# A convolution's zeroing, round change and skip rebuilt, and a first projection started ahead of its rates

## The chip, the core and the metric

One core of a Trainium2 chip runs the whole program. Its engines are TensorE (PE, with its weight loads shown as PEld), VectorE (DVE), ScalarE (ACT), GpSimd (POOL) and SyncE (SP), which issues all DMAs here. The metric is the device time of one execution in microseconds, the median of the runs. PE's granted clock is shown as a share of 2.4 GHz.

## What is computed

Cut to what matters here: 16 images of 64 channels and 32 x 32 pixels go through a two-sided recurrent convolution of 32 steps, then through a state-space scan, then through a mixture of experts.

```python
# convolution: 32 steps for a left and a right side, f = 32 features
pre = sigmoid(s2s(h, w, b, shift) + x @ w_i2s)   # o, fg, ig, g = split(pre, 4)
c = fg * c + ig * g
h = o * tanh(c)
...
x1 = x + (lh + shift_down(rh)) @ w_skip + b_skip
# scan: layernorm of x1, projections xs, z, delta, Bv, Cv
state = exp(delta * A) * state + delta * Bv * xs
y = (state @ C) * silu(z) @ W_out
```

## The kernel before

**The convolution** (`conv_phase`) keeps four streams s: two sides times two halves of the batch group, four images (GROUP) in each. `rows[s]` holds 64 channels of state (rows 0 to 63, the previous features twice, shifted) above 64 channels of x. There are two rounds, each of 8 images, 32 steps and four streams per step. For each stream PE computes the four gates of two chunks (512 pixels) with 16 matmuls a chunk in quarters of its columns (L165), ACT applies the sigmoid (L207) and tanh (L214), POOL and DVE update the cell (L247, L270, L277), DVE writes the features (L285) and SP copies them into `rows` (L136). After 32 steps the skip runs: for each of 8 images and 2 chunks PE multiplies both sides' features with `skip_w` (L180, L182) into rows 64 to 127 of one PSUM bank, DVE adds bias and x (L307), SP stores (L143).

Before the first round POOL and DVE zero all of `rows` and `feat` (L228, L229, L253, L254); at the start of each round, the first one too, SP loads x (L129) in the order 0, 2, 1, 3, POOL zeroes the state rows of streams 0, 2 and 1 (L237, L240), DVE the cells and stream 3 (L263, L264), and PE waits for all of it once (L151). The loops over rounds are loops of the machine (Fori) on every engine.

**The scan phase** (`build_scan`) starts when all engines have left the convolution. The projection of one batch is a list of 16 stages (STAGES, L505): MEAN, VARIANCE, two OWN, two RATES, two READOUT, STEPS_OF, OWN_TOKENS and ENTERS twice, two Z. In each, PE fills one PSUM bank `work_ps` (`fill`), ACT drains it (`drain`), and where the value is split into bf16 parts, ACT takes the first and second part and POOL the remainders (L1111, L1115); SP stores the parts (`store_stage`). The two buffers `parts` are used by turns: ACT's first part of a stage waits (`parts_out`) until the stores of the last stage but one of that kind have landed. Batch 0 is projected ahead of everything; the later ones run inside the scan of the batch before. Ahead of batch 0's projection the rates A are turned (L728), split into three bf16 parts by ACT and DVE (L919 to L923, L1211, L1214), stored and loaded back (L611, L620). POOL and DVE zero the scan's tiles (L1070 to L1074, L1206 to L1209). When the last stage's parts are stored, SP loads the first span (`load`, L622), and the scan begins (DVE L1231).

All order between engines comes from semaphores written out by hand; each engine's own order is the program's.

## Time and profile before

| what | us |
|---|---|
| median of 3 runs | 6596.51 (6596.5 to 6597.06) |
| the profiled execution | 6594.51 |
| its span, first to last instruction | 6592.7 |
| PE busy | 6199.5 (94%) |
| DVE busy | 6099.6 (93%) |
| ACT busy | 4496.3 (68%) |
| POOL busy | 2566.4 (39%) |

The busy shares are means over phases with different limits, so they are read phase by phase. The convolution ends at about 1886 us, the scan phase at about 6504 us; the experts take the rest. A busy PE counts matmuls that overlap.

### The profile page before, as it was taken

How to read it: one execution, taken by the hardware profiler on the slowest of the kernel's cores; microseconds unless marked ns; L12 is line 12 of the kernel's file. 1: busy time of each engine (PE TensorE's matmuls, PEld its weight loads, DVE VectorE, ACT ScalarE, POOL GpSimd, SP SyncE). 2: the span in 40 equal slices, each digit the busy share in tenths (PEclk: the TensorE clock that was granted, in tenths of full speed). 3: DMA queues.
4: the chain of work that ended last, by engine and by line, in shares of the span. 5: the costliest groups of instructions: out<-in, count | busy, mean ns of one | idle time of the engine just before them, and what ended most of it. 6: DMA issues, size and time to landing. Idle time of an engine off the chain costs nothing. (4 is left out here: it accounts for less than half of the span.)

```text
span 6592.7 us, 155525 instructions
## 1 busy us (share of the span) xinstructions
PE 6199.5 (94%) x52289; PEld 4017.0 (61%) x52289; DVE 6099.6 (93%) x3714; ACT 4496.3 (68%) x9595; POOL 2566.4 (39%) x7016
## 2 busy tenths in 40 slices
PE   8999989999959999999999999999999999999996
PEld 3666634567726666666666666666666666666654
DVE  7888878888839999999999999999999999999995
ACT  7888858888836666666666666666666666666662
POOL 5555545555532333333333333333333333333321
PEclk9999999999979999999999999999999999999997
DMA  6666666666641221212212122221212212222114
GB/s 144 154 154 154 154 145 154 154 154 154 155 105 44 49 56 40 65 47 52 55 41 63 42 59 49 47 58 38 68 46 51 55 41 64 48 53 50 45 32 127
DMA packets 904175, 538.20 MB, mean 82 GB/s; under 512 B 695565, under 2 KB 813997, under 8 KB 903597
## 3 DMA queue, kind: packets, MB, share of 16 engines
q1 hardware_dynamic: 903597, 531.10, 34.5%
q8 instruction: 289, 4.73, 0.3%
q14 instruction: 289, 2.37, 0.1%
HBM read 142.32 MB, written 107.35 MB: 38 GB/s over the span
## 5 line engine op out<-in xcount | busy, mean ns | idle before, releaser
L1231 DVE TENSOR_TENSOR_SCAN states<-decay,enter_ps 128x1024 f32<-128x1024 f32 x2048 | 4471.9, 2262 | 86.3 <-PE enter_ps L801 73.6
L987 ACT ACTIVATE decay<-rate_ps 128x512 f32<-128x512 f32 (+1 forms) x4096 | 2221.7, 594 | 344.0 <-PE rate_ps L787 149.0
L801 PEld LDWEIGHTS enter_ps<-s_steps,s_tokens 128*128 128x128 bf16 x16384 | 1602.8, 129 | 1358.6 <-DVE states L1231 1063.0
L801 PE MATMUL enter_ps<-s_steps,s_tokens 128*128 128x128 bf16 x16384 | 2142.1, 310 | 238.1 <-DVE states L1231 228.3
L787 PE MATMUL rate_ps<-s_wide,s_decays 128*128 128x256 bf16 x8192 | 1318.5, 283 | 4.8 <-DMA s_wide<-rates_dram 4.5
L247 POOL TENSOR_TENSOR entered<-gates 128x512 f32<-128x512 f32 x512 | 901.1, 1760 | 887.5 <-ACT gates L207 887.5
L1167 POOL TENSOR_TENSOR product<-decay,states 128x16 f32<-128x16 f32 x1920 | 465.8, 243 | 1788.0 <-ACT decay L987 1784.4
L994 ACT COPY enter_ps<-at_first 128x16 f32<-128x16 f32 x1920 | 337.5, 176 | 1188.0 <-PE enter_ps L801 1134.2
L831 PE MATMUL y_ps<-states,spread 128*32 128x512 f32 x8192 | 1090.3, 604 | 2.4 <-issue 2.4
L165 PE MATMUL pre<-rows,weights_left 128*32 128x512 f32 x8192 | 909.1, 595 | 36.0 <-POOL rows L240 23.8
L787 PEld LDWEIGHTS rate_ps<-s_wide,s_decays 128*128 128x128 bf16 x8192 | 903.5, 118 | 63.4 <-issue 6.1
L285 DVE TENSOR_TENSOR feat<-gates,squashed 128x512 f32<-128x512 f32 x512 | 904.0, 1766 | 1.4 <-ACT squashed L214 1.4
L165 PE MATMUL pre<-rows,weights_right 128*32 128x512 f32 x8192 | 904.9, 593 | 0.0
L165 PEld LDWEIGHTS pre<-rows,weights_left 128*32 128x32 f32 x8192 | 541.6, 109 | 381.6 <-issue 217.8
L165 PEld LDWEIGHTS pre<-rows,weights_right 128*32 128x32 f32 x8192 | 549.0, 109 | 334.5 <-issue 175.6
L207 ACT ACTIVATE gates<-pre,biases_left 128x512 f32<-128x512 f32 x1024 | 620.4, 689 | 133.9 <-PE pre L165 133.9
L207 ACT ACTIVATE gates<-pre,biases_right 128x512 f32<-128x512 f32 x1024 | 620.7, 689 | 125.0 <-PE pre L165 125.0
L270 DVE TENSOR_TENSOR forgot<-gates,cell 128x512 f32<-128x512 f32 x512 | 356.7, 697 | 260.1 <-ACT gates L207 259.9
L1172 POOL TENSOR_TENSOR at_first<-at_first,product 128x16 f32<-128x16 f32 x1920 | 426.5, 222 | 309.9 <-ACT at_first L1002 309.9
L277 DVE TENSOR_TENSOR cell<-forgot,entered 128x512 f32<-128x512 f32 x512 | 347.4, 678 | 2.3 <-POOL entered L247 2.3
L214 ACT ACTIVATE squashed<-cell 128x512 f32<-128x512 f32 x512 | 330.8, 646 | 5.6 <-DVE cell L277 5.6
L831 PEld LDWEIGHTS y_ps<-states,spread 128*32 128x32 f32 x8192 | 161.6, 107 | 219.6 <-issue 219.6
(136 smaller groups left out, 2487.9 us busy)
## 6 DMA issues: line engine op xcount, KB each, us to landing
rows<-feat SPq DMA_DIRECT2D x1024, 132.0 KB, 2.4
rows<-feat SPq DMA_DIRECT2D x512, 128.0 KB, 2.4
s_steps<-steps_dram SPq DMA_DIRECT2D x4096, 8.0 KB
rows<-feat SPq DMA_DIRECT2D x512, 127.8 KB, 2.4
s_wide<-rates_dram SPq DMA_DIRECT2D x1024, 32.0 KB, 1.9
s_tokens<-tokens_dram SPq DMA_DIRECT2D x2048, 16.0 KB, 2.1
rates_dram<-parts SPq DMA_DIRECT2D x64, 384.0 KB, 3.3
steps_dram<-parts SPq DMA_DIRECT2D x64, 384.0 KB, 3.5
```

Source lines behind the costliest of these rows:

```text
L165: mm = pe.matmul(pre[c][32 * q:32 * q + 32, g, :], weights[side(s)][:, 32 * g:32 * g + 32], image(rows[s][:, q, :], MARGIN + CIMG * c), st ...
L207: a = act.activation(gates[k % GATE_RING][:, g, :], pre[k % CHUNKS][:, g, :], ACT.Sigmoid, bias=biases[side(k // CHUNKS)][:, g:g + 1])
L247: pool.tensor_tensor(entered[c][:, :], gates[k % GATE_RING][:, 2, :], gates[k % GATE_RING][:, 3, :], ALU.mult).then_inc(entered_ready, 1)
L270: dve.tensor_tensor(forgot[c][:, :], gates[k % GATE_RING][:, 1, :], cell[s][:, BANK * c:BANK * c + BANK], ALU.mult).then_inc(forgot_ready, 1)
L285: dve.tensor_tensor(image(feat[s][:, :], CIMG * c), gates[k % GATE_RING][:, 0, :].rearrange("p (h w) -> p h w", w=SIDE), squashed[c][:, :] ...
L787: mm = pe.matmul(rate_ps[h][:, QUAD * q:QUAD * q + QUAD, :], decays[:, g, 2 * h + q, :], wide[s][:, g, :, :], start=True, stop=True)
L801: mm = pe.matmul(out.rearrange("p h l -> p l h"), tokens[s][:, k, :], steps[s][:, k, :, d:d + half], start=True, stop=True)
L831: mm = pe.matmul(y_ps[32 * j:32 * j + REACH, :].rearrange("p (r d) -> p d r", r=QUAD), spread[s][:, at:at + REACH], steps_of.rearrange("p ...
L987: act.activation(decay[i][:, half, at:], rate_ps[h][:, :, at:], ACT.Exp).then_inc(decay_ready, 1)
L1167: pool.tensor_tensor(product[i][:, :], decay[g % RING][:, :, 0], states[set_of(c - 1)][:, mine, SPAN - 1], ALU.mult).then_inc(product_read ...
L1172: pool.tensor_tensor(at_first[set_of(c)][:, mine], at_first[set_of(c)][:, mine], product[i][:, :], ALU.add).then_inc(added, 1)
L1231: dve.tensor_tensor_scan(out, factor, term, 0.0, ALU.mult, ALU.add).then_inc(scanned, 1)
```

## The change

In the convolution: SP loads stream 0's x first, then the weights, then the other x, without waiting for any zeroing; the round loop on SP is written out. Before the first round only the margins of the x rows and the state rows are zeroed, and the round's zeroing stands at the end of the round instead of its start: the cells before the skip's evacuations, state rows of streams 0 and 2 after half of them, of 1 and 3 after all. PE waits for each stream's zeroing with a semaphore of its own, in the step loop. The skip takes an image's two chunks into the two column halves (rows 64 to 127 and 0 to 63) of two banks, with the matmuls of the two interleaved. ACT does one small sigmoid at the start of each round.

In the scan phase: mean_w and batch 0's x are loaded first; PE fills MEAN before it turns the rates and before it waits for the other weights; ACT splits the rates after the first drain; all the scan's zeroing goes to DVE, behind the rates, and is waited for where the scan begins; batch 0's stages use `work_ps` and `rate_ps[0]` by turns, so that a fill waits for the drain of the last stage but one (RATES and VARIANCE for all drains).

```diff
@@ -81,7 +81,11 @@
...
-        weights_in, zeroed, state_zeroed = sem("weights_in"), sem("zeroed"), sem("state_zeroed")
+        warm = sb("warm", [128, 1])
+        weights_in, zeroed, cells_zeroed, margins_zeroed = (
+            sem("weights_in"), sem("zeroed"), sem("cells_zeroed"), sem("margins_zeroed"))
+        state_zeroed = [sem(f"state_zeroed{s}") for s in range(STREAMS)]
...
+        def skip_ps(k, c):
+            at = CH * (1 - c)
+            return pre[k % 2][at:at + CH, c, :]
...
+            def load_x(r, s):
+                if r:
                     sp.wait_ge(x1_ready, START + r * SKIPS - (1 - half(s)) * SKIPS // 2)
-                    src = x_pad[bass.ds((r * 2 + half(s)) * GROUP, GROUP), :, :].rearrange("q c p -> c q p")
...
+                first = (r * 2 + half(s)) * GROUP
+                sp.dma_start(rows[s][CH:128, :, MARGIN:MARGIN + IMG], x_pad[first:first + GROUP, :, :].rearrange(
+                    "q c p -> c q p")).then_inc(x_in[s], DMA)
+            def load_weights():
+                for d, s in ((weights[0], w_left), (weights[1], w_right), (biases[0], bias_left),
+                             (biases[1], bias_right), (skip_w[0], w_skip_left), (skip_w[1], w_skip_right)):
+                    sp.dma_start(d[:, :], s).then_inc(weights_in, DMA)
+                sp.dma_start(skip_b[CH:128, :], b_skip).then_inc(weights_in, DMA)
+            for r in range(ROUNDS):
+                if r == 0:
+                    load_x(r, 0)
+                    load_weights()
+                    for s in (1, 2, 3):
+                        load_x(r, s)
+                else:
+                    for s in (0, 2, 1, 3):
+                        load_x(r, s)
...
+            pe.wait_ge(margins_zeroed, START + 1)
             with pe.Fori(0, ROUNDS) as r:
-                pe.wait_ge(state_zeroed, START + (r + 1) * 2)
-                pe.sem_inc(passed, 1)
...
+                        pe.wait_ge(state_zeroed[s], START + r + 1)
...
-                for k in range(SKIPS):
-                    h, q, c = k // (GROUP * CHUNKS), k // CHUNKS % GROUP, k % CHUNKS
-                    if q == 0 and c == 0:
+                for k in range(SKIPS // CHUNKS):
+                    h, q = k // GROUP, k % GROUP
+                    if q == 0:
                         for s in (h, 2 + h):
                             pe.wait_ge(rows_in[s], START + (r + 1) * STEPS * MOVES * DMA)
-                    if k >= 4:
-                        pe.wait_ge(x1_ready, START + r * SKIPS + k - 3)
-                    out = pre[k // 2 % 2][CH:128, k % 2, :]
-                    pe.matmul(out, skip_w[0][:, :], image(rows[h][:, q, :], MARGIN + 1 + CIMG * c),
-                              start=True, stop=False)
-                    pe.matmul(out, skip_w[1][:, :], image(rows[2 + h][:, q, :], MARGIN - 1 + CIMG * c),
-                              start=False, stop=True).then_inc(skip_ready, 1)
+                    if k >= 2:
+                        pe.wait_ge(x1_ready, START + r * SKIPS + (k - 1) * CHUNKS)
+                    for c in range(CHUNKS):
+                        pe.matmul(skip_ps(k, c), skip_w[0][:, :], image(rows[h][:, q, :], MARGIN + 1 + CIMG * c),
+                                  start=True, stop=False)
+                    for c in range(CHUNKS):
+                        pe.matmul(skip_ps(k, c), skip_w[1][:, :], image(rows[2 + h][:, q, :], MARGIN - 1 + CIMG * c),
+                                  start=False, stop=True).then_inc(skip_ready, 1)
...
+                act.activation(warm[:, :], biases[0][:, 0:1], ACT.Sigmoid)
...
+            pool.memset(rows[0][0:CH, :, :], 0.0).then_inc(state_zeroed[0], 1)
+            pool.memset(rows[1][0:CH, :, :], 0.0).then_inc(state_zeroed[1], 1)
+            pool.wait_ge(state_zeroed[1], START + 1)
             for s in range(2):
-                pool.memset(rows[s][:, :, :], 0.0)
...
-                pool.wait_ge(x1_ready, START + r * SKIPS - SKIPS // 2)
-                pool.sem_inc(passed, 1)
-                for s in (0, 2):
-                    pool.memset(rows[s][0:CH, :, :], 0.0)
-                pool.wait_ge(x1_ready, START + r * SKIPS)
-                pool.sem_inc(passed, 1)
-                pool.memset(rows[1][0:CH, :, :], 0.0).then_inc(state_zeroed, 1)
...
+                pool.wait_ge(x1_ready, START + (r + 1) * SKIPS - SKIPS // 2)
+                pool.sem_inc(passed, 1)
+                for s in (0, 2):
+                    pool.memset(rows[s][0:CH, :, :], 0.0).then_inc(state_zeroed[s], 1)
+                pool.wait_ge(x1_ready, START + (r + 1) * SKIPS)
+                pool.sem_inc(passed, 1)
+                pool.memset(rows[1][0:CH, :, :], 0.0).then_inc(state_zeroed[1], 1)
...
+            for s in range(STREAMS):
+                dve.memset(rows[s][CH:128, :, 0:MARGIN], 0.0)
+                z = dve.memset(rows[s][CH:128, :, MARGIN + IMG:], 0.0)
+            z.then_inc(margins_zeroed, 1)
+            dve.memset(rows[2][0:CH, :, :], 0.0).then_inc(state_zeroed[2], 1)
+            dve.memset(rows[3][0:CH, :, :], 0.0).then_inc(state_zeroed[3], 1)
...
                 z = dve.memset(feat[s][:, :], 0.0)
             z.then_inc(zeroed, 1)
+            def zero_cells():
+                for s in range(STREAMS):
+                    z = dve.memset(cell[s][:, :], 0.0)
+                z.then_inc(cells_zeroed, 1)
+            zero_cells()
...
-                for s in range(STREAMS):
-                    dve.memset(cell[s][:, :], 0.0)
-                dve.memset(rows[3][0:CH, :, :], 0.0).then_inc(state_zeroed, 1)
-                dve.wait_ge(state_zeroed, START + (r + 1) * 2)
-                dve.sem_inc(passed, 1)
...
+                zero_cells()
...
-                        in0=pre[k // 2 % 2][CH:128, k % 2, :].rearrange("p (h w) -> p h w", w=SIDE),
+                        in0=skip_ps(k // CHUNKS, c).rearrange("p (h w) -> p h w", w=SIDE),
...
+                dve.wait_ge(x1_ready, START + (r + 1) * SKIPS)
+                dve.sem_inc(passed, 1)
+                dve.memset(rows[3][0:CH, :, :], 0.0).then_inc(state_zeroed[3], 1)
...
+        def bench(b, n):
+            return work_ps if b or n % 2 == 0 else rate_ps[0][:, :, :].rearrange("p h l -> p (h l)")
...
+            def load_x(b):
+                sp.wait_ge(centred_ready, SCAN0 + b)
+                sp.sem_inc(passed, 1)
+                sp.dma_start(px[:, :], by_half(x1_dram)[b, :, :, :].rearrange("k c l -> (k c) l")).then_inc(x_in, DMA)
+            sp.dma_start(wmean[:, :], mean_w).then_inc(mean_in, DMA)
+            load_x(0)
+            sp.dma_start(rate_t[:, :], a_t).then_inc(consts_in, DMA)
+            sp.dma_start(ident[:, :], identity).then_inc(consts_in, DMA)
+            for d, s in ((wdelta, w_delta), (wc, w_c)):
...
-            load_x(0)
-            sp.dma_start(rate_t[:, :], a_t).then_inc(consts_in, DMA)
-            sp.dma_start(ident[:, :], identity).then_inc(consts_in, DMA)
...
-            sp.wait_ge(pool_zeroed, SCAN0 + 1)
-            sp.wait_ge(vector_zeroed, SCAN0 + 1)
+            sp.wait_ge(decays_zeroed, SCAN0 + 1)
...
+            sp.wait_ge(vector_zeroed, SCAN0 + 1)
...
-            pe.wait_ge(consts_in, SCAN0 + 2 * DMA)
-            pe.wait_ge(y_zeroed, SCAN0 + 1)
-            pe.transpose(y_ps[:, 0:128], rate_t[:, :], ident[:, :]).then_inc(turned, 1)
-            pe.wait_ge(weights_in, SCAN0 + WEIGHTS * DMA)
-            pe.wait_ge(by_place_set, SCAN0 + 1)
...
+                work_ps = bench(b, n)
+                pe.wait_ge(drained, stages_to(b, n) if b or kind in (RATES, VARIANCE) else stages_to(b, max(n - 1, 0)))
...
+            pe.wait_ge(mean_in, SCAN0 + DMA)
             for n in range(len(STAGES)):
                 fill(0, n)
+                if n == 0:
+                    pe.wait_ge(consts_in, SCAN0 + 2 * DMA)
+                    pe.wait_ge(y_zeroed, SCAN0 + 1)
+                    pe.transpose(y_ps[:, 0:128], rate_t[:, :], ident[:, :]).then_inc(turned, 1)
+                    pe.wait_ge(weights_in, SCAN0 + WEIGHTS * DMA)
+                    pe.wait_ge(by_place_set, SCAN0 + 1)
                 fill_inverse(0, n)
+            pe.wait_ge(drained, stages_to(1, 0))
...
-            pe.wait_ge(pool_zeroed, SCAN0 + 1)
...
-            act.wait_ge(turned, SCAN0 + 1)
-            act.copy(rate[:, :], y_ps[:, 0:128]).then_inc(rate_moved, 1)
-            act.wait_ge(rate_moved, SCAN0 + 1)
-            act.copy(rate_parts[:, 0, :], rate[:, :]).then_inc(rate1, 1)
-            act.wait_ge(left1, SCAN0 + 1)
-            act.copy(rate_parts[:, 1, :], rate_left[:, :]).then_inc(rate2, 1)
-            act.wait_ge(vector_zeroed, SCAN0 + 1)
...
+            def split_rates():
+                act.wait_ge(turned, SCAN0 + 1)
+                act.copy(rate[:, :], y_ps[:, 0:128]).then_inc(rate_moved, 1)
+                act.wait_ge(rate_moved, SCAN0 + 1)
+                act.copy(rate_parts[:, 0, :], rate[:, :]).then_inc(rate1, 1)
+                act.wait_ge(left1, SCAN0 + 1)
+                act.copy(rate_parts[:, 1, :], rate_left[:, :]).then_inc(rate2, 1)
...
+                if n == 0:
+                    split_rates()
+            act.wait_ge(vector_zeroed, SCAN0 + 1)
...
-            pool.memset(steps[0][:, :, :, :], 0.0)
-            pool.memset(decays[:, :, :, :], 0.0)
-            for s in range(SETS):
-                pool.memset(room[s][:, INNER * SPAN:], 0.0)
-                z = pool.memset(spread[s][:, :], 0.0)
-            z.then_inc(pool_zeroed, 1)
-            pool.wait_ge(pool_zeroed, SCAN0 + 1)
...
+            pool.wait_ge(vector_zeroed, SCAN0 + 1)
...
+            dve.memset(decays[:, :, :, :], 0.0).then_inc(decays_zeroed, 1)
...
-            for i in range(RING):
-                dve.memset(decay[i][:, :, :], 0.0)
-            for s in range(SETS):
-                dve.memset(wide[s][:, :, :, :], 0.0)
-            dve.memset(steps[1][:, :, :, :], 0.0).then_inc(vector_zeroed, 1)
...
+            for i in range(RING):
+                dve.memset(decay[i][:, :, :], 0.0)
+            for s in range(SETS):
+                dve.memset(wide[s][:, :, :, :], 0.0)
+                dve.memset(steps[s][:, :, :, :], 0.0)
+                dve.memset(room[s][:, INNER * SPAN:], 0.0)
+                z = dve.memset(spread[s][:, :], 0.0)
+            z.then_inc(vector_zeroed, 1)
+            dve.wait_ge(consts_in, SCAN0 + 2 * DMA)
+            rows = ident[:, :].rearrange("p (j a e) -> p j a e", j=4, a=2)
+            for a in range(2):
+                p = dve.tensor_scalar(place[:, SPAN * a:SPAN * a + SPAN].rearrange("p (j e) -> p j e", e=16), rows[:, :, a, :],
+                                      0.5, None, ALU.mult)
+            p.then_inc(placed, 1)
...
```

## Rows read from the trace of the kernel before

**Rows 1.** Busy time of each engine (instructions) in three stretches, granted clock, DMA share, GB/s.
```profile
1000.00:1800.00 800.00, 800.00 (x7424) 509.25 (x7416) 692.07 (x696) 682.40 (x1160) 408.16 (x233) 1.00 0.68 154
1921.10:1965.50 44.40, 28.65 (x64) 14.67 (x64) 0.00 (x0) 14.83 (x27) 18.29 (x16) 0.50 0.38 123
2000.00:6500.00 4500.00, 4256.55 (x35050) 2830.82 (x35047) 4456.01 (x2041) 2933.83 (x6939) 1592.38 (x6453) 1.00 0.21 50
```

**Rows 2.** Timeline of the start: start us, us, engine, line, operation, idle before.
```profile
2.23 0.39 SPq L121 DMA_DIRECT2D weights_left<-w_left  x1
...
19.40 3.62 POOL L240 MEMSET rows<- 64x4240 f32 x1
...
23.76 8.76 PE L165 MATMUL pre<-rows,weights_left 128*32 128x512 f32 x64 [23.76 <-POOL rows L240]
...
29.20 1.28 ACT L207 ACT_TABLE_LOAD   x1 [29.20 <-PE pre L165]
...
30.50 4.74 ACT L207 ACTIVATE gates<-pre,biases_left 128x512 f32<-128x512 f32 x8
...
32.97 7.10 PE L165 MATMUL pre<-rows,weights_left 128*32 128x512 f32 x64 [0.46 <-ACT gates L207]
```

**Rows 3.** x's loads in the first 45 us; DMA traffic of 20 to 34.
```profile
DMA to landing us min/median/max: 8.1/14.9/21.5
...
DMA packets 702, 2.83 MB, mean 202 GB/s; under 512 B 32, under 2 KB 32, under 8 KB 702
```

**Rows 4.** Timelines by engine of the first skip and the round change.
```profile
918.03 1.94 PE L180 MATMUL pre<-rows,skip_w_left 128*64 128x512 f32 x2 [8.39 <-DMA rows<-feat]
...
957.80 9.35 PE L165 MATMUL pre<-rows,weights_left 128*32 128x512 f32 x64 [10.41 <-DMA rows<-x_pad]
968.48 7.08 PE L165 MATMUL pre<-rows,weights_left 128*32 128x512 f32 x64 [1.33 <-DMA rows<-x_pad]
...
921.79 0.76 DVE L307 SCALAR_TENSOR_TENSOR x<-pre,skip_b,rows 64x512 f32<-64x512 f32 x1 [5.28 <-PE pre L182]
...
947.43 0.76 DVE L307 SCALAR_TENSOR_TENSOR x<-pre,skip_b,rows 64x512 f32<-64x512 f32 x1 [0.96 <-PE pre L182]
...
953.53 3.59 DVE L264 MEMSET rows<- 64x4240 f32 x1 [0.82 <-issue]
...
949.46 3.07 SPq L129 DMA_DIRECT2D rows<-x_pad  x4
```

**Rows 5.** Timelines: the second skip's end, the scan phase's first, an output product.
```profile
1882.89 0.76 DVE L307 SCALAR_TENSOR_TENSOR x<-pre,skip_b,rows 64x512 f32<-64x512 f32 x1 [0.96 <-PE pre L182]
...
1886.56 0.11 POOL L1067 MEMSET power<- 128x8 f32 x1 [36.87 <-POOLq L65]
...
2342.56 1.08 PE L851 MATMUL stage_ps<-gated,wout 128*64 128x512 f32 x4
```

**Rows 6.** Timelines by engine of the scan phase's front.
```profile
1913.07 1.84 PE L745 MATMUL stage_ps<-wmean,square 128*128 128x2 f32 x8 [10.68 <-POOL square L1089]
...
1921.08 2.07 PE L752 MATMUL stage_ps<-normed,win 128*128 128x512 f32 x2 [2.02 <-POOL normed L1103]
...
1909.36 0.23 DVE L1211 TENSOR_TENSOR rate_left<-rate,rate_parts 128x128 f32<-128x128 f32 x1
...
1982.42 2.29 DVE L1231 TENSOR_TENSOR_SCAN states<-decay,enter_ps 128x1024 f32<-128x1024 f32 x1 [71.91 <-PE enter_ps L801]
...
1963.60 0.36 SPq L577 DMA_DIRECT2D tokens_dram<-parts  x1
```

**Rows 7.** Groups by line in 1921:1966; DMA issues in 1890:1985, median us to landing.
```profile
L1115 POOL TENSOR_TENSOR parts<-rest,parts 128x512 bf16<-128x512 f32 x6 | 6.9, 1154 | 4.4 <-ACT parts L973 4.4
...
L961 ACT COPY moved<-stage_ps 128x512 f32<-128x512 f32 x7 | 4.1, 588 | 4.5 <-PE stage_ps L757 4.5
...
px<-x_dram SPq DMA_DIRECT2D x2, 256.0 KB, 2.7
...
steps_dram<-parts SPq DMA_DIRECT2D x2, 256.0 KB, 3.8
```

30 lines of the change are left out of this document (10 added, 20 removed).

## The prediction, made before the changed kernel ran

> **What bounds the kernel now.** I read the busy shares by stretch first [rows 1]. In the convolution's steady part PE is busy 800.00 of 800 us at a granted clock of 1.00 (2.4 GHz): PE sets the pace. In the scan DVE is busy 4456 of 4500 us. Between these lies the first batch's projection, 44.4 us in which no engine is busy two thirds of the time and the granted clock is 0.50 (1.2 GHz). So the two long stretches can't be shortened by this change, which leaves their instructions alone but for one wait; what it can move are the serial pieces between them. The timelines of those give four: the start [rows 2, 3], the round change with its skip [rows 4], the same skip again before the scan [rows 5], and the scan's front [rows 6, 7]. All four are serial, so what one loses or gains shifts everything behind it.
>
> **1. The start.** PE's first matmul is at 23.76, released by POOL's last zeroing (19.40 + 3.62) [rows 2]. That chain goes: both engines zero whole rows, SP waits for them, x is loaded, and only the round's own zeroing, repeated over the same rows, lets PE go. After the change, SP loads x for stream 0 first. Its present first issue is at 2.23 [rows 2]; five more semaphores are set up in front of it, each below 0.1 us, so 2.5. The earliest x load of the four took 8.1 us from issue to landing and the last 21.5 [rows 3], so the four share the queues one behind the other, about 5.3 us each at the 202 GB/s shown. Stream 0 lands at 10.6. The seven weight loads are queued behind it: 0.2 MB at the same rate, about 1 us, ending at 11.6 to 12.5. The zeroing in front of PE is now one half-height memset on POOL (3.62, over by 4.4) and the margins on DVE: PE starts at about **11.8**, on weights instead of on POOL. Streams 1, 2, 3 land at about 17, 22, 28; PE wants them at 20.4, 27, 34 (its first pieces are 8.6 and then 6.9 us long [rows 2]). DVE's zeroing (14,700 elements a partition at 3.59 per 4240 [rows 4], 12.4 us, and gaps between eight memsets) ends near 18, before the first gates at 11.8 + 5.4 + 2.4 = 19.6. The table load of 1.28 us [rows 2] moves ahead of PE's first result; now PE's second stream starts 9.21 us after the first because it waits for ACT; without the load it would be bound by its own 8.6, so 0.6 comes back and not 1.28. Gain 12.0 + 0.5 = **12.5**, ends 10.5 and 13.5.
>
> **2. The first skip.** It runs from 918.03; its first evacuation is at 921.79 and its 16th ends at 948.19, one each 1.71 us, each waiting for PE [rows 4]. PE computes the two halves of an image in turn, in 64 of its columns. The change puts them on different column halves and interleaves them. The nearest row is the scan's output product, which writes both column halves too: four matmul instructions of this size in 1.08 us [rows 5], where the skip needs 1.71 for four. So two halves should cost PE 1.71 instead of 3.42. The other engine becomes nearly as tight: a group's two evacuations need 2 x 0.76, and group k waits for those of group k-2. That cycle is 1.93 (8 instructions) + 1.52 + 0.14 (a wait on another engine) + whatever gap lies between two evacuations, for two groups: 1.8 each without a gap; with the largest gap DVE shows with nothing to wait for, 0.82 [rows 4], 2.2. I take 1.8, as the gap is shown before a memset of another shape. The x1 stores have a ring of four, land 2.3 us after issue and need a pace of 1.7 per group or slower: they just fit. The first group stays at the low clock (3.43 for what then takes 1.71). So group 7 starts at 918.0 + 3.4 + 6 x 1.8 = 932.3 and the last evacuation ends at 935.8: gain **12.3** (9.5 to 13).
>
> A rule of the Trainium skill speaks of the evacuations: by "VectorE: DVE Perf Modes", section "Two Vector instructions with no wait between them", an instruction whose PSUM input starts in another quadrant than the last one's is held until all earlier ones have ended. The new evacuations alternate between partitions 64 and 0, so all would be held. No row shows it; it would only fill the gap that the range above already contains.
>
> **3. The round change.** Now: last evacuation 948.19, x loads issued at 949.46, PE at 957.80 released by the landing, second stream at 968.48 released by the third landing [rows 4]. The change takes the zeroing out of the way (cells in the 5 us in which DVE waits for the skip's first product, streams 0 and 2 during the skip's second half, streams 1 and 3 afterwards, 3.6 to 4.7 us against 9.6 until x lands), but PE waits for the load and not for it. So nothing of the zeroing is gained here, and the table load is not gained either: PE's second stream waits for a landing 10.68 us after the first, whatever ACT does. All is shifted by the skip's 12.3, **0** beside it (-0.5 to +1.5).
>
> **4. The second skip and the end of the phase.** The same 12.3. But the moved zeroing is now at the end of every round, also of the last. Now the phase ends with the last store's landing: evacuation over at 1883.65, scan phase at 1886.56, 2.9 us [rows 5]. After: DVE's stream 3 memset comes behind the last evacuation, 0.4 for the wait, up to 0.82 of idle and 3.59 [rows 4], so 4.7, and about 0.5 for the barrier: 5.1. Cost 2.2 (1 to 3). Net **10.1**.
>
> **5. The scan's front to the second stage.** Now all weights, then x, then the rates' constants are loaded; PE turns the rates first, and ACT can drain the first mean only after DVE's zeroing (rate_left at 1909.36), so PE's variance matmul comes at 1913.07, 26.5 us into the phase [rows 6]. After: mean_w and x are loaded first, and PE's mean starts about 8 us in (x issued at 5.3, landing 2.7 later [rows 7]). Drain, centring and squaring end at 13.2. In PE's order the wait for the remaining weights now stands between mean and variance. The last of 14 loads is issued at 11.2, lands 2.2 later, the by_place copy takes 0.3: variance at **13.9**. Gain 12.6. Behind that wait nothing else is queued but the transpose's successors; ACT's second rate copy waits for DVE, over by 14.4, before the variance is there at 15.7. SP's 19 decay loads are finished 24 us in, the first parts store is due at 33. From variance to the first OWN product the chain is unchanged, 8.0 us [rows 6]. DVE's zeroing, 15,600 elements a partition, 13.2 us at the same rate and 17 with gaps, now runs 15 to 32 us in; it is wanted at 60. Its cost is nil unless it slows POOL beside it; no row has a POOL operation beside a DVE memset, the nearest is POOL's memset of [rows 2], at 3.62 no slower than without company: 0, at worst 2.
>
> **6. Two banks.** OWN at zero, the last third part (what SP stores and the loads wait for) ends now 42.4 after it (OWN at 1921.08, store of the last part at 1963.60) [rows 6]. With two banks PE fills the next stage while ACT drains. I laid the stages out from [rows 7]: PE 2.05 per stage at the low clock, 1.71 back to back; ACT 0.59 a copy; POOL 1.15 each. OWN1 starts at 1.7 and ends its drain at 4.4; the rates stages still wait for all drains, 4.55 and 7.85; the readouts are drained at 13.4 and 13.9; STEPS_OF 0 is cast at 15.6 and its third part is ready at 19.9; ENTERS 0 is stored at 25.0. Then a new wait: STEPS_OF 1 takes the parts buffer whose three stores were issued from 20.0 on, the last landing 3.8 after its issue [rows 7], at 24.7, where ACT would be free at 23.8. Its chain goes on through 27.0 (rest), 28.1 (ENTERS 1 drained), plus the 5.8 that its six operations on ACT and POOL, 0.6 to 1.3 each with the hand-overs, take now: 33.9. Gain **8.6**; 6 if POOL is slowed, 9.5 if the stores land sooner. PE is by then busy nearly without gaps, and a rise of the clock would give under 1 us, since ACT, POOL and the stores hold the chain. From the store to the first scan nothing changes (1963.60 to 1982.42, 18.8 us of store, landing and SP's issues).
>
> **7. The added wait in the step loop.** PE waits once more for each stream, 256 times, and DVE once per round. Behind it on PE is the stream's first matmul, behind that ACT, POOL and DVE. Today two or three waits stand at the same place and PE has no idle time there [rows 1], so I take 0. If nothing hid it, it would be some 0.1 us, 26 in all.
>
> **Sum.** 12.5 + 12.3 + 0 + 10.1 + 12.6 + 8.6 = 56.1 us. The profiled execution took 6594.51 (span 6592.7 and 1.8 around it): 6538.4. The median of the runs, 6596.51, lies 2.0 higher, so I forecast **6540.5**.
>
> **Rivals.** (a) The column halves don't overlap. Then both skips keep 1.71 per half and 24.6 is lost: 6565. For it: the weights change with each matmul; against it the 1.08 us of [rows 5]. The Trainium skill would have it so: "TensorE: Matmul & The Clock Gate", section "Part 3: Packing small matmuls — row/col tiling", says that a weight load overlaps running matmuls only when its row group differs, and here all use the full rows. The trace disagrees: in the four-column-group matmuls of the step loop PE is busy without idle time although each has its weight load [rows 1]. Chance 0.03. (b) The projection gains less (POOL slowed by DVE's memsets, or stores that hold both parts buffers): 12 instead of 21, 6550. Chance 0.1. (c) It ends slower: the added wait empties PE's queue, so that each stream's first matmul starts only when the last one has ended. That costs one matmul's time less its pitch, 0.6 - 0.1 = 0.5 us, 256 times: 128 us, 6668. It decides from 0.27 us per wait on. Against it: the waits there already don't do so. Chance 0.02. (d) The same wait is hidden in part, 5 to 25 us: 6546 to 6566, 0.04. (e) The convolution's part does not do what it says, because the weights land late behind x or the phase's end costs more: 6545, within my range, 0.06.
>
> **Chances and range.** The forecast, 6533 to 6549, has 0.75. Adding up the ends of the terms, with (b) and part of (d), gives **6530 to 6558** for 8 in 10. A measurement of this kernel can tell 0.2% (13 us) from no change; all cases but (c) and the worst of others are beyond it: faster 0.96, same 0.02, slower 0.02.
>
> **What would show it.** PE's first matmul near 11.8, released by a weights DMA. In each skip, pairs of evacuations 0.8 apart, every 1.8 us, and 18 us from first skip matmul to last evacuation. x landings 8 us after the stores as now. The phase's end 5 us after the last evacuation, with a DVE memset in it. Variance 14 us and OWN 22 us into the scan phase, the last parts store at 56, the first scan at 75. PE without idle time in the step loop. It would be wrong if PE idled at stream changes, if evacuations stayed 1.7 us apart, or if the gain in the projection were taken by waits for parts stores.

## The result and the profile after

The changed kernel takes 6540.72 us (median of 4 runs, 6538.69 to 6541.35) against 6596.78 us for the kernel before on the same chip (4 runs, 6596.5 to 6597.44): a ratio of 0.9916, 95% interval 0.9904 to 0.9928, so 56.1 us less. The profiled execution took 6541.35 us, with a span of 6539.6. The profiled span before was 6592.7, so the two traces differ by 53.1 us and not by 56.1: the one of before lay 2.3 us under its median, the one of after 0.6 above. Everything below that is read from traces adds up to 53, not 56.

The table follows the difference through the program. A mark is a moment in both traces, in us from the span's start. The last column is what the stretch ending at the mark gave. Each column is one trace: how far such marks scatter is told at the head of the experiments, and a difference below about 1 us in a stretch is not a finding.

| mark | before | after | ahead by | this stretch |
|---|---|---|---|---|
| PE's first matmul | 23.76 | 13.66 | 10.10 | 10.10 |
| first skip, first matmul | 918.03 | 907.18 | 10.85 | 0.75 |
| first skip, last evacuation over | 948.19 | 925.51 | 22.68 | 11.83 |
| second skip, first matmul | 1853.71 | 1831.46 | 22.25 | -0.43 |
| second skip, last evacuation over | 1883.65 | 1850.15 | 33.50 | 11.25 |
| first work of the scan phase | 1886.56 | 1855.09 | 31.47 | -2.03 |
| variance matmul | 1913.07 | 1868.88 | 44.19 | 12.72 |
| last parts store | 1963.60 | 1910.30 | 53.30 | 9.11 |
| first scan | 1982.42 | 1929.06 | 53.36 | 0.06 |

**The start**, against [rows 2, 3]. The first four lines are from the timeline, the next two from the DMA issues of the first 16 us (size, and median time from issue to landing), the last the one x load issued in the window 2.4 to 3.2:

```profile
2.50 0.76 SPq L133 DMA_DIRECT2D rows<-x_pad  x1
...
6.34 0.51 SPq L140 DMA_DIRECT2D skip_b<-b_skip  x1
...
12.96 1.28 ACT L240 ACT_TABLE_LOAD   x1 [12.96 <-DMA skip_b<-b_skip]
...
13.66 2.79 PE L186 MATMUL pre<-rows,weights_left 128*32 128x512 f32 x12 [13.66 <-DMA skip_b<-b_skip]
...
weights_left<-w_left SPq DMA_DIRECT2D x1, 64.0 KB, 7.3
...
skip_b<-b_skip SPq DMA_DIRECT2D x1, 0.2 KB, 6.5
...
rows<-x_pad SPq DMA_DIRECT2D x1, 1056.0 KB, 8.0
```

PE is now released by a weights DMA and not by POOL. Stream 0's x is issued at 2.50 and takes 8.0, so it lands at 10.5; the last weight is issued at 6.34 and takes 6.5, for 0.2 KB. It lands at 12.8, and PE's first matmul follows 0.85 later. PE then runs 128 matmuls in a row, where it stood idle for 0.46 us before its second stream [rows 2].

**The first skip and the round change**, against [rows 4]. First the busy times by engine in three windows (columns as in [rows 1]), then lines of the timeline by engine:

```profile
905.00:912.00 7.00, 4.82 (x12) 1.66 (x14) 5.29 (x7) 1.44 (x2) 0.00 (x0) 0.51 0.84 193
912.00:926.00 14.00, 11.94 (x54) 3.26 (x50) 11.06 (x15) 0.00 (x0) 7.53 (x3) 1.00 0.62 133
926.00:935.00 9.00, 0.00 (x0) 0.00 (x0) 3.59 (x1) 0.00 (x0) 3.29 (x1) 0.67 0.94 192
...
907.18 1.98 PE L201 MATMUL pre<-rows,skip_w_left 128*64 128x512 f32 x4 [8.39 <-DMA rows<-feat]
...
914.78 1.08 PE L201 MATMUL pre<-rows,skip_w_left 128*64 128x512 f32 x4
915.70 1.03 PE L204 MATMUL pre<-rows,skip_w_right 128*64 128x512 f32 x4
...
915.02 1.54 DVE L342 SCALAR_TENSOR_TENSOR x<-pre,skip_b,rows 64x512 f32<-64x512 f32 x2 [0.29 <-PE pre L204]
916.75 1.54 DVE L342 SCALAR_TENSOR_TENSOR x<-pre,skip_b,rows 64x512 f32<-64x512 f32 x2 [0.20 <-PE pre L204]
...
935.33 9.01 PE L186 MATMUL pre<-rows,weights_left 128*32 128x512 f32 x64 [11.39 <-DMA rows<-x_pad]
946.02 7.08 PE L186 MATMUL pre<-rows,weights_left 128*32 128x512 f32 x64 [1.68 <-issue]
```

A group of four matmuls now takes 1.08 us as in the output product of [rows 5], and the evacuations come in pairs (1.54 for two). From the third pair (915.02) to the eighth (923.97) they are 1.6 to 2.0 us apart, 1.79 in the mean. Until 912 the granted clock is 0.51. PE's next start still waits for x, and its second stream comes 10.69 us after the first (10.68 before).

**The end of the convolution and the front of the scan phase**, against [rows 5, 6]: lines of the timeline, then two windows.

```profile
1847.00 3.15 DVE L342 SCALAR_TENSOR_TENSOR x<-pre,skip_b,rows 64x512 f32<-64x512 f32 x4 [0.51 <-PE pre L204]
...
1851.21 3.59 DVE L350 MEMSET rows<- 64x4240 f32 x1 [1.06 <-issue]
1855.09 0.11 POOL L1119 MEMSET power<- 128x8 f32 x1 [1.16 <-POOLq L65]
...
1868.88 1.84 PE L784 MATMUL rate_ps<-wmean,square 128*128 128x2 f32 x8 [3.37 <-DVE by_place L1249]
...
1891.81 0.59 ACT L991 CAST parts<-stage_ps 128x512 bf16<-128x512 f32 x1 [2.14 <-DMA rates_dram<-parts]
1900.94 0.59 ACT L991 CAST parts<-rate_ps 128x512 bf16<-128x512 f32 x1 [1.08 <-DMA steps_dram<-parts]
...
1910.30 0.36 SPq L623 DMA_DIRECT2D tokens_dram<-parts  x1
...
1000.00:1780.00 780.00, 780.00 (x7236) 467.78 (x7231) 674.70 (x679) 664.90 (x1130) 398.11 (x226) 1.00 0.68 154
1868.00:1911.00 43.00, 24.13 (x88) 14.89 (x88) 16.61 (x19) 15.86 (x30) 20.50 (x18) 0.73 0.44 138
```

A DVE memset now stands between the last evacuation and the scan phase. Variance is released by `by_place`, the last consumer of the weight loads. In the projection ACT waits twice for a store of parts that it wants to overwrite. The granted clock is 0.73 there; it was 0.50 [rows 1].

### The profile page after: what moved, and what is told of

Read it like the earlier page. It is cut to its first block and busy times, and to the rows that moved or that the text cites. A ratio compares the mean times of both kernels' runs of the same rounds, so it can differ in the third digit from the quotient of the medians.

```text
span 6539.6 us, 155482 instructions
## 1 busy us (share of the span) xinstructions
PE 6169.2 (94%) x52289; PEld 3694.8 (56%) x52289; DVE 6112.0 (93%) x3734; ACT 4495.5 (69%) x9597; POOL 2554.8 (39%) x7010
## 3 DMA queue, kind: packets, MB, share of 16 engines
q14 instruction: 289, 2.37, 0.1%
## 5 line engine op out<-in xcount | busy, mean ns | idle before, releaser
L186 PEld LDWEIGHTS pre<-rows,weights_left 128*32 128x32 f32 x8192 | 389.4, 109 | 524.2 <-issue 439.4
L186 PEld LDWEIGHTS pre<-rows,weights_right 128*32 128x32 f32 x8192 | 389.4, 109 | 494.0 <-issue 401.4
L1214 POOL MEMSET decay<- 128x16 f32 x1920 | 242.3, 126 | 113.5
```

Of the source, the lines that this page charges most:

```text
L186: mm = pe.matmul(pre[c][32 * q:32 * q + 32, g, :], weights[side(s)][:, 32 * g:32 * g + 32], image(rows[s][:, q, :], MARGIN + CIMG * c), st ...
```

## The experiments

All medians are of timed runs of a kernel beside the kernel before on the same chip (whose medians were 6594.4 to 6596.8 in the five groups of runs). Where only 1 to 3 us are at stake I judge by marks in the trace. The reason is in the runs themselves: the stretch from the first scan to the end, which no experiment touches, took between 4607.9 and 4614.7 us in the fourteen traces.

Marks scatter too, by less. In the ten traces whose start is the changed kernel's, PE's first matmul comes at 13.66 to 14.54 us; the changed kernel's own trace has the earliest. From there to the first skip the thirteen traces of changed kernels take 893.5 to 895.3 us (before: 894.3), a skip that no experiment touched 17.3 to 18.9, and the eight with SP's loads of x and the skip as changed take 922.9 to 924.6 from the first skip's first matmul to the second's. So I count a stretch between two marks, and not a mark from the span's start, and call less than about 1 us scatter unless it comes back in several traces.

**E1: both chunks of an image in one column half.** The changed kernel with the skip's outputs in partitions 64 to 127 of both banks.

```diff
-            at = CH * (1 - c)
-            return pre[k % 2][at:at + CH, c, :]
+            return pre[k % 2][CH:128, c, :]
```

> The changed kernel, but both halves of an image are written to partitions 64 to 127 (two banks, matmuls still interleaved, evacuations still wait by groups). Theory: the skips' gain is the overlap of the two column halves on PE. Then a group costs PE 3.4 us again, each skip takes about 30 us from first matmul to last evacuation (18.3 and 18.7 in the changed kernel), and the time is 23 us above the changed kernel, about 6564. Rival: the gain came from the interleaving and the two buffers, not from the columns; then each skip stays below 22 us and the time rises by less than 8 us.

Measured: 6566.87 us (6564.46 to 6568.88), ratio 0.9957 (0.9943 to 0.9971). The timeline of its first skip, PE then DVE:

```profile
914.11 1.89 PE L200 MATMUL pre<-rows,skip_w_left 128*64 128x512 f32 x4
915.83 1.88 PE L203 MATMUL pre<-rows,skip_w_right 128*64 128x512 f32 x4
...
916.89 1.61 DVE L341 SCALAR_TENSOR_TENSOR x<-pre,skip_b,rows 64x512 f32<-64x512 f32 x2 [1.82 <-PE pre L203]
920.44 1.50 DVE L341 SCALAR_TENSOR_TENSOR x<-pre,skip_b,rows 64x512 f32<-64x512 f32 x2 [1.94 <-PE pre L203]
```

Four matmuls now start 1.72 apart from the next four, where the changed kernel has 0.86 to 0.92, and each pair of evacuations waits 1.8 to 1.9 us for PE. The skip, from first matmul to last evacuation, takes 31.1 us (908.03 to 939.13) in place of 18.3. The column halves are the whole of the skip's gain: by the marks 24.5 us for both rounds (31.1 and 30.4 us against 18.3 and 18.7); the medians differ by 26. The order of the matmuls is that of the changed kernel, and the skip of before took 30.2 us, so interleaving alone brought nothing. Whether the column halves would do it without interleaving was not run.

**E2: one bank for the stages.** All of batch 0's stages in `work_ps`, each fill behind the last drain.

```diff
-            return work_ps if b or n % 2 == 0 else rate_ps[0][:, :, :].rearrange("p h l -> p (h l)")
+            return work_ps
...
-                pe.wait_ge(drained, stages_to(b, n) if b or kind in (RATES, VARIANCE) else stages_to(b, max(n - 1, 0)))
+                pe.wait_ge(drained, stages_to(b, n))
```

> The changed kernel with batch 0's stages in one bank again, each fill waiting for all drains. Theory: two banks are worth what the trace shows between the first OWN product and the last parts store (42.5 us before, 33.4 after): the stretch is 42.5 again, the time 9 us above the changed kernel, about 6550. Rival: the stretch got shorter because PE's clock rose in it; then it is the clock and not the bank that matters, and the stretch stays below 38 us with the time less than 5 us up.

Measured: 6550.03 us (6549.16 to 6553.39), ratio 0.9935 (0.9918 to 0.9951). The window of its projection, and its last store:

```profile
1868.00:1920.00 52.00, 30.97 (x87) 18.08 (x88) 15.78 (x19) 15.93 (x29) 20.31 (x18) 0.50 0.37 115
...
1919.68 0.36 SPq L623 DMA_DIRECT2D tokens_dram<-parts  x1
```

From OWN (1877.16) to the last store are 42.5 us; before it was 42.5 too, after 33.4. So the two banks give 9.1 us, and the rest of the front nothing of it. The clock stays at 0.50, so the rise to 0.73 came with the two banks, and the 9.1 us hold what the clock gave: E2 takes both away together.

**E3: the small weights ahead of x in the scan phase's front.**

```diff
-            load_x(0)
-            sp.dma_start(rate_t[:, :], a_t).then_inc(consts_in, DMA)
-            sp.dma_start(ident[:, :], identity).then_inc(consts_in, DMA)
...
+            load_x(0)
+            sp.dma_start(rate_t[:, :], a_t).then_inc(consts_in, DMA)
+            sp.dma_start(ident[:, :], identity).then_inc(consts_in, DMA)
```

> The changed kernel with the scan phase's x and the rates' constants loaded behind all weights, as before the change; only mean_w stays in front. Theory: of the 12.7 us that the variance matmul comes earlier, the load order is worth the smaller part: x is issued 10.4 us in, lands at 13.1, and mean, drain, centring and squaring (5.2 us) end at 18.5 against 13.8 now, so plus 4.7 us, about 6545; the other 8 us come from ACT no longer waiting for DVE's zeroing. Rival: the load order is the whole gain, plus 12 us, about 6553.

Measured: 6545.06 us (6544.17 to 6546.05), ratio 0.9926 (0.9909 to 0.9943). In its timeline:

```profile
1868.53 2.07 PE L779 MATMUL stage_ps<-px,wmean 128*128 128x512 f32 x2 [19.59 <-DMA px<-x_dram]
...
1873.94 1.83 PE L784 MATMUL rate_ps<-wmean,square 128*128 128x2 f32 x8 [3.12 <-POOL square L1133]
```

Variance comes 23.4 us after the last evacuation (1850.52), against 18.7 in the changed kernel: 4.7 later, and it is now released by POOL's square instead of by `by_place`. So of the front's 12.7 us, 4.7 come from the order of the loads; the other 8.0 are left to what E3 keeps, the mean ahead of the rates and DVE's zeroing out of the way. I didn't separate those two.

**E4 and E4b: the added wait.** E4 has the wait for `state_zeroed` three times in the step loop. E4b takes it out of the loop and puts four waits ahead of the round.

```diff
                         pe.wait_ge(state_zeroed[s], START + r + 1)
+                        pe.wait_ge(state_zeroed[s], START + r + 1)
+                        pe.wait_ge(state_zeroed[s], START + r + 1)
```

> The changed kernel with the new wait in PE's step loop issued three times in a row, 512 more waits. Theory: PE's sequencer runs ahead of the matmuls, so the wait is free: same time within 1.5 us, about 6541, and no idle time of PE in the step loop. Rival: the wait costs what its issue takes, about 0.1 us each: plus 50 us, and then the change itself pays 25 us for it. Second rival: it empties the queue: plus 250 us.

> The changed kernel with TensorE's added wait taken out of the step loop and put once ahead of the round. Theory: the wait in the loop costs nothing, since three of it cost nothing: 6540 to 6541.5, TensorE busy 780.00 of 780 us between 1000 and 1780. Rival: one wait in the loop already costs what three do not add to, and without it the time falls below 6538.

Measured: E4 6540.07 us (6539.53 to 6546.17), E4b 6541.29 us (6538.19 to 6542.18), the changed kernel 6540.72. The same window of E4, then of E4b:

```profile
1000.00:1780.00 780.00, 780.00 (x7238) 482.57 (x7234) 674.89 (x679) 664.23 (x1131) 397.77 (x226) 1.00 0.68 154
```

```profile
1000.00:1780.00 780.00, 780.00 (x7236) 454.33 (x7232) 674.87 (x679) 664.96 (x1131) 397.67 (x226) 1.00 0.68 154
```

No wait in the loop, one or three: PE is busy throughout and does the same number of matmuls, to within 2 of 7236. The wait is free. Neither rival has anything left.

**E5: no zeroing after the last round.** The round loops of POOL and DVE written out, and left before the zeroing when no round follows.

```diff
-                zero_cells()
+                if r + 1 < ROUNDS:
+                    zero_cells()
...
+                if r + 1 == ROUNDS:
+                    break
```

> The changed kernel, with the zeroing of features and cells left out behind the last round (nothing reads them there). Theory: the zeroing at the phase end, 3.6 us on VectorE and GpSimd side by side behind the last evacuation (1850.15 to 1855.09 in the changed kernel's trace), is what the second skip gives back, so without it the scan phase starts 2 to 4.5 us earlier and the time is 2 to 4.5 us under the changed kernel's 6540.7: 6536 to 6539, and the stretch from the last evacuation to the first work of the scan phase falls from 4.9 to about 1.0 to 2.5 us. Rival: the phase end is bounded by SyncE's drain or the barrier and not by the zeroing; then the time stays within 1 us of 6540.7.

Measured: 6536.49 us (6530.19 to 6538.25), ratio 0.9908 (0.9891 to 0.9925). Its timeline at the end of the convolution:

```profile
1847.29 1.54 DVE L345 SCALAR_TENSOR_TENSOR x<-pre,skip_b,rows 64x512 f32<-64x512 f32 x2 [0.18 <-PE pre L204]
1851.55 0.11 POOL L1124 MEMSET power<- 128x8 f32 x1 [24.11 <-POOLq L65]
```

From the last evacuation's end (1848.83) to the scan phase's first work are 2.7 us, 4.9 in the changed kernel and 2.9 before. So the zeroing is what the second skip gives back, 2.2 us. The stretch didn't fall to 1.0 to 2.5 as I expected: it is what it was before, and what I read there as the last store's landing. The median is 4.2 lower, of which the trace explains half.

**E6: three buffers for parts.**

```diff
-        parts = [sb(f"parts{i}", [128, SPLITS, BANK], BF16) for i in range(2)]
+        parts = [sb(f"parts{i}", [128, SPLITS, BANK], BF16) for i in range(3)]
```

> The changed kernel with three buffers for the projection's parts in place of two. Theory: ScalarE's two waits for a part's store (2.14 us at 1891.81 and 1.08 us at 1900.94 in the changed kernel's trace) stand on the path from the last part to the first scan; with a third buffer they go, and the last tokens' store and the first scan come 2 to 3 us earlier: 6537.5 to 6539. Rival: the loads and matmuls behind it are next in line (a load of rates or steps, or TensorE at its low clock), and the time is 6540 to 6541, the waits having moved to another releaser.

Measured: 6539.04 us (6538.0 to 6541.41), ratio 0.9914 (0.9898 to 0.9931). In its trace:

```profile
1868.00:1911.00 43.00, 25.76 (x88) 14.49 (x88) 14.79 (x19) 15.85 (x30) 21.29 (x18) 0.66 0.47 146
...
1891.34 0.59 ACT L991 CAST parts<-stage_ps 128x512 bf16<-128x512 f32 x1 [0.82 <-PE stage_ps L796]
...
1908.97 0.36 SPq L623 DMA_DIRECT2D tokens_dram<-parts  x1
```

Both waits for stores are gone, 3.2 us of them, but from OWN (1876.66) to the last store are 32.3 us against 33.4: 1.1 came through. It is not scatter: the three traces with three buffers (E6, E9, E10) take 32.26 to 32.31, the nine with two buffers and two banks 33.0 to 34.5. In the place of the first wait stands one of 0.82 us for PE. Another 1.1 us were lost ahead of it: ACT drains the first readout 12.8 us after OWN and not 11.7, with the granted clock at 0.50 over the first 12 us behind OWN, where it is above 0.8 in the changed kernel. So the theory is right about the place and too high in size; most of the rest of the 3.2 us went to PE, as the rival has it.

**E7 and E8: the two loads that the new kernel waits for.** E8 issues the seven small weights from ACT and x from SP.

```diff
+            for d, s in ((weights[0], w_left), (weights[1], w_right), (biases[0], bias_left),
+                         (biases[1], bias_right), (skip_w[0], w_skip_left), (skip_w[1], w_skip_right)):
+                act.dma_start(d[:, :], s).then_inc(weights_in, DMA)
+            act.dma_start(skip_b[CH:128, :], b_skip).then_inc(weights_in, DMA)
```

> The changed kernel, with the seven small weight loads issued by ScalarE's queue at the start and the four of x by SyncE's. Theory: the first matmul (13.66 us) waits for the last weight, which lands 2.3 us after x because it stands behind it in one issuing queue; with two issuers the weights land with x or before it and the first matmul comes 1 to 1.5 us earlier: 6539 to 6540. Rival: the seven loads share the 16 DMA engines with x either way and x itself lands later by as much; the first matmul is at 13 to 14.5 us and the time at 6540.5 to 6542.

Measured: 6537.55 us (6536.85 to 6538.71), ratio 0.9912 (0.9896 to 0.9929). In its trace, issues first:

```profile
3.58 0.55 ACTq L217 DMA_DIRECT2D skip_b<-b_skip  x1
...
13.65 2.79 PE L178 MATMUL pre<-rows,weights_left 128*32 128x512 f32 x12 [13.65 <-DMA skip_b<-b_skip]
...
weights_left<-w_left ACTq DMA_DIRECT2D x1, 64.0 KB, 1.9
...
skip_w_right<-w_skip_right ACTq DMA_DIRECT2D x1, 32.0 KB, 7.0
...
skip_b<-b_skip ACTq DMA_DIRECT2D x1, 0.2 KB, 9.2
```

The median would have passed for my theory; the trace refutes it. The first five weights land in about 2 us. The last two, issued at 3.10 and 3.58, behind x's 2.51 but in another engine's queue, take 7.0 and 9.2 (a second load of x is issued at 3.32, between the two), and skip_b lands at 12.8 just as in the changed kernel. PE starts at 13.65 instead of 13.66. That is not quite nothing, since the changed kernel's 13.66 is the earliest of ten traces (the middle is 14.2) and E9 and E10, with the same edit, have 13.78 and 13.81: perhaps 0.4 us, not the 1 to 1.5 of the theory. The 3 us of the median are mostly the long part behind, 4607.85 us here, the shortest of the fourteen. So a small load behind a 1 MB load waits for most of it, whoever issues it. The Trainium skill says so in "DMA: Bandwidth & Descriptors", section "Issuing engines are not separate DMA queues": loads of different engines run on the same 16 DMA engines and interleave. This trace agrees that the issuer does not matter; of interleaving the last two loads saw little (skip_w_right lands at 10.1, x at 10.7). I had cost that queue by bytes alone.

E7 has the second round's x issued by ACT during the skip instead of by SP behind the skip's stores; for that PE waits for the last evacuation before it begins the round. The two kernels differ in the order of the four streams only, 0, 1, 2, 3 and 0, 2, 1, 3.

```diff
+                if r + 1 < ROUNDS:
+                    for s in (0, 1, 2, 3):
+                        act.wait_ge(x1_ready, START + (r + 1) * SKIPS - (1 - half(s)) * SKIPS // 2)
+                        first = ((r + 1) * 2 + half(s)) * GROUP
+                        act.dma_start(rows[s][CH:128, :, MARGIN:MARGIN + IMG], x_pad[first:first + GROUP, :, :].rearrange(
+                            "q c p -> c q p")).then_inc(x_in[s], DMA)
```

> The changed kernel, with the second round's x loaded from ScalarE's queue while the skip runs (streams in the order 0, 1, 2, 3), in place of SyncE's loads behind the round's end. Theory: TensorE's start of round 2 waits for x (first matmul at 935.33, 9.3 us after x is asked for at 926.02), and its second stream waits for its own x until 946.02. With the loads issued during the skip, the second stream's x is there about 10 us earlier, so round 2 gains 8.5 to 11 us: 6530 to 6532. Rival 1: the round's start is bounded by the zeroing and the barrier just as closely, and only 0 to 3 us are gained (6538 to 6541). Rival 2: x's 1 MB loads beside the skip slow the skip's own operands or evacuations, and half of the gain is given back (6535 to 6537).

> As the kernel with x loaded during the skip in the order 0, 1, 2, 3 (6534.75 us), but in the order 0, 2, 1, 3. Theory: in the new round the streams run in the order 0, 1, 2, 3, so with stream 1's x third in the queue its first step is held until the third landing, some 2.5 to 3 us later per load in the queue: 6536 to 6538. Rival: all loads land before they are needed, and the order makes no difference: 6534 to 6535.5.

Measured: with 0, 1, 2, 3 6534.75 us (6533.15 to 6537.14), ratio 0.9908 (0.9892 to 0.9925); with 0, 2, 1, 3 6537.08 us (6534.45 to 6543.26), ratio 0.991 (0.9894 to 0.9927). First lines of the former, then of the latter:

```profile
928.17 3.10 DVE L347 SCALAR_TENSOR_TENSOR x<-pre,skip_b,rows 64x512 f32<-64x512 f32 x4 [4.66 <-DMA x_dram<-x]
...
932.52 16.31 PE L183 MATMUL pre<-rows,weights_left 128*32 128x512 f32 x128 [6.92 <-issue]
```

```profile
929.27 0.76 DVE L347 SCALAR_TENSOR_TENSOR x<-pre,skip_b,rows 64x512 f32<-64x512 f32 x1 [6.75 <-DMA x_dram<-x]
...
935.17 15.95 PE L183 MATMUL pre<-rows,weights_left 128*32 128x512 f32 x128 [10.55 <-issue]
```

The second stream's wait is gone in both (128 matmuls in a row). But the skip itself is longer: its last four evacuations wait for the buffers that hold x on its way out, because these stores now move beside a 1 MB load. With one load beside them the wait is 4.66 us and the skip ends at 931.27; with two (streams 0 and 2 before the last stores) it is 6.75 and 1.6 more, and the skip ends at 933.92, against 925.51. From the first skip's first matmul to the second's the two take 917.2 and 921.5 us, against 922.9 to 924.6 in the eight traces with SP's loads: about 6 and 2 us less. So my second rival was right, half of the gain is given back, and the order matters, but not for the reason I gave: no stream waits for its landing.

**E9 and E10: everything together.** E9 has the edits of E5, E6, E8 and E7 (order 0, 1, 2, 3). E10 is E9 with eight buffers for the skip's output.

```diff
-OUT_RING = 4
+OUT_RING = 8
```

> The changed kernel with four edits together: no zeroing behind the last round, three buffers for parts, the second round's x (streams 0, 1, 2, 3) loaded by ScalarE's queue during the skip, and the small weights issued by ScalarE at the start. Theory: the edits lie in four separate places of one chain (start, round change, phase end, head of the scan phase), so their gains add. Alone they took 6540.7 to 6536.5, 6539.0, 6534.8 and 6537.6: 4.2, 1.7, 5.9 and 3.1 us, together 14.9 us: 6524 to 6529. Rival: two of them meet the same limit (the parts' buffers only move the wait to TensorE or a load; single gains of 2 to 3 us are partly scatter), and the sum is 8 to 11 us: 6530 to 6533.

> The kernel with the four edits together (6531.1 us), and eight buffers for the skip's output in place of four. In its trace the last four evacuations of the skip wait 5.09 us for a store of x that moves beside the next round's x load, and round 2 starts only at 931.78. Theory: the store wait is what gave back half of the gain of the early load. With eight buffers the last evacuation ends at about 925.5 in place of 930.5, stream 1's x is asked for 5 us earlier, and round 2 starts when stream 0's x has landed, about 929 to 931: 1 to 3 us less, 6528 to 6530. Rival: the load and the stores share one limit of bytes, so the wait only moves to stream 0's x or to the last loads, and the time stays within 1 us of 6531.

Measured: E9 6531.13 us (6530.04 to 6534.21), ratio 0.9904 (0.9888 to 0.9921); E10 6526.46 us (6523.59 to 6528.73), ratio 0.9895 (0.9878 to 0.9911). Adding single medians misled me for E9; the marks add up. Its first scan is at 1920.02, 9.0 us ahead of the changed kernel's, where E5's 2.2, E6's 1.1 and E7's 5.3 (second skip's end at 1844.86 against 1850.15) make 8.6, an agreement within the scatter of such marks. Lines of E9, then of E10:

```profile
927.43 3.10 DVE L346 SCALAR_TENSOR_TENSOR x<-pre,skip_b,rows 64x512 f32<-64x512 f32 x4 [5.09 <-DMA x_dram<-x]
...
931.78 16.02 PE L175 MATMUL pre<-rows,weights_left 128*32 128x512 f32 x128 [7.44 <-issue]
...
931.70:941.00 9.30, 9.22 (x68) 2.51 (x72) 4.17 (x2) 2.62 (x5) 3.51 (x2) 0.77 1.02 205
```

```profile
925.67 1.54 DVE L346 SCALAR_TENSOR_TENSOR x<-pre,skip_b,rows 64x512 f32<-64x512 f32 x2 [0.31 <-PE pre L193]
...
928.61 7.09 PE L175 MATMUL pre<-rows,weights_left 128*32 128x512 f32 x64 [2.96 <-DMA rows<-x_pad]
...
x_dram<-x SPq DMA_DIRECT2D x14, 128.0 KB, 4.6
...
928.60:938.00 9.40, 8.57 (x80) 2.62 (x84) 4.63 (x3) 4.78 (x9) 4.10 (x2) 1.00 1.05 243
```

With eight buffers the evacuations wait for PE alone. The stores are no faster: the eight beside the load take 4.3 to 7.5 us to land, the others 2.2 to 2.3 (the 4.6 above is the median of all fourteen in its window), and E9's four beside the load took 5.8 to 7.6. PE starts at stream 0's landing. The first skip of this trace began 1.0 us later than E9's (909.11 against 908.07), so I count from there: PE starts round 2 after 19.5 us, 4.2 sooner than in E9, and the third stream 5.2 sooner. The 1.0 between is the clock, net: PE was idle for 3.0 us instead of 7.4, the granted clock stayed at 1.00, and the first 64 matmuls took 7.09 us (9.01 in the changed kernel), while the second stream now waits 0.8 us for its x. I had expected 1 to 3 us, and the first scan is 4.9 sooner (1915.12), 5.9 counted from the first skip; the last 0.7 is within the scatter. From the first skip to the second it is 912.9 us, 10 to 12 less than with SP's loads: the 8.5 to 11 that E7's theory gave to the early load come with eight buffers. E10 beats both kernels, by 14 us the changed one (medians of different groups of runs; the first scans differ by 13.9).

## Why the prediction was right, step by step

The forecast was 6540.5 and the median 6540.72. The closeness is partly luck: the steps summed to 56.1 and the medians differ by 56.1, but the steps are read in traces, and these differ by 53.1. The 3 us between are in how the profiled executions lie to their medians.

- **1, the start: 12.0 and 0.5 forecast, 10.1 and 0.75 measured, the step mis-sized most.** Stream 0's x landed as worked out (10.5 against 10.6). "0.2 MB at the same rate, about 1 us, ending at 11.6 to 12.5" was too short: the last weight landed 2.3 us behind x. The seven loads landed 0.2 to 0.6 us apart, those of 2 KB no closer together than those of 64 KB, so each cost about the same whatever its bytes. The second miss is that I let PE start at the landing; 0.74 us pass before and 0.85 after between the release and its first matmul (POOL's zeroing over at 23.02 and PE at 23.76 in [rows 2]; 12.81 and 13.66 after). And 10.1 is the best of ten traces, the others have 9.2 to 9.8. The 0.5 for the table load is right in kind (the idle of 0.46 us before the second stream is gone in every trace), but its 0.75 from first matmul to first skip can't be told from scatter: the thirteen changed traces lie on both sides of the one before.
- **2 and 4, the skips: 12.3 each forecast, 11.83 and 11.25 measured.** The pace per group was right (1.8; measured 1.77 to 1.90 from the fourth group on), the column halves overlap (E1, 24.5 us), and the gap between the two evacuations of a pair is 0.03 us. What failed is "the first group stays at the low clock": the second did too, in part, 2.37 us in place of 1.8. The Trainium skill's rule on held instructions ("VectorE: DVE Perf Modes", section "Two Vector instructions with no wait between them") would fill a gap that hardly exists: with alternating halves the second evacuation of a pair starts 0.79 us after the first, of 0.756 us. That agrees with the rule, by which it starts only when the first has ended, and costs 0.03 us a pair. E1 can't show what a pair without the rule takes, since its second evacuations end their wait with PE.
- **The phase's end: 2.2 forecast, 2.03 measured**, and E5 took 2.2 of it away.
- **3, the round change: 0 forecast, -0.43 measured.** PE starts 9.3 us after x is asked for instead of 8.3; second stream and table load as said.
- **5, the front: 12.6 forecast, 12.72 measured.** Variance came 13.8 us into the phase (13.9 forecast), on `by_place` as said; 4.7 of it is the order of the loads (E3), the other 8.0 were not split.
- **6, two banks: 8.6 forecast, 9.11 measured.** The new wait for a parts store is where it was forecast (STEPS_OF 1, 24.1 us after OWN, 1.08 us; forecast 24.7, 0.9 us), and a second one that I didn't foresee (STEPS_OF 0, 2.14 us). Why the stretch was still shorter than forecast is not shown. The clock, whose gain I had put under 1 us, is one candidate. In the nine traces with two banks and two buffers it averages 0.67 to 0.80 from OWN to the last store and the stretch takes 33.0 to 34.5 us, 33.9 at the lowest (E5), so within this range it moved about 1 us at most; what two banks would give at 0.50 no run shows.
- **7, the added wait: 0 forecast, 0 measured** (E4, E4b).

The rivals: column halves that don't overlap is refuted by the pace and by E1, which is that case and came within 2 us of the 6565 worked out for it. With the Trainium skill's "only" for weight loads of another row group, in "TensorE: Matmul & The Clock Gate", section "Part 3: Packing small matmuls — row/col tiling", the trace disagrees: weights change with every matmul here, all with full rows, and four still take 1.08 us. The rival read too much into that sentence, for a table in the same section gives outputs in different columns a measured gain too. The rival of the projection gaining less is out by the marks (12.7 and 9.1 us) and E2, the two of the added wait by E4. The fifth, weights that land late, is what happened in small.

## What to carry to other kernels

Between two long stretches that are each bound by one engine, the serial pieces add: cost each by its own marks, and judge an edit of 1 to 3 us by the stretch between the marks around it and not by the median, which here moved 3 us for an edit worth some 0.4 (E8). One pair of traces is not enough below 1 us: the same start came at 13.66 to 14.54. If a small operand gates the first work, load it ahead of the large transfer, since another queue doesn't help it: in E8 the weights issued ahead of x, or 0.1 us behind it, landed in 2 us and those further behind in 7 to 9. What all seven ahead of x would give was not run, and where the large load gates the work the order has to be the other one (E3, 4.7 us). And if a load is moved beside stores, give the stores' ring more buffers, or the gain comes back as a wait for them. Where an M of 64 leaves half of the columns idle, put two outputs on the two halves: a group of eight matmuls went from 3.43 us to about 1.8 and the product from 30.2 to 18.3, because PE and not the evacuation had set its pace.

## What the runs showed of the hardware that was not expected

- A load of 32 KB issued 0.6 us after one of 1 MB, from another engine, took 7.0 us to land, and one of 0.2 KB that also stood behind a second of 1 MB took 9.2; the five issued before them took 1.7 to 2.0 (E8).
- Stores of 128 KB issued behind such a load took 4.3 to 7.5 us to land instead of 2.2 to 2.3 (E10).
- After 3.0 us without matmuls PE's granted clock stayed at 1.00 (2.4 GHz); after 7.4 it averaged 0.77 over the next 9.3 us, which is time at each of the two levels of 1.2 and 2.4 GHz (E10, E9).
- Two more semaphore waits at each of the 256 stream changes cost PE nothing (E4), and reading PSUM at the other half of the partitions left 0.03 us between two evacuations (the changed kernel).
